# Gated delta rule layer: another partition order for the triangular solver, and the static product's first chunk one place later on TensorE

## The reference, cut to what matters

```python
# x: (8, 2048, 256); 16 heads of 16; W: (256, 256); FFN hidden 768, int weights / 127
x_act = tanh(x)
static_out = einsum('bld,ed->ble', x_act, W)
q = k = to_heads(x_act); v = to_heads(static_out)
# per head: S = lam*S; u = beta*(v_t - S^T k_t); S += k_t u^T; o_t = S^T q_t
y = static_out + o
x = layernorm(x + layernorm(y) * ln_gamma + ln_beta)
x = layernorm(x + ffn(x))          # ffn: (silu(x Wg) * (x Wu)) Wd
```

## Time and profile before

| | before |
|---|---|
| runs | 1788.28, 1783.09, 1778.01 us; median 1783.09 us |
| profiled execution | 1788.68 us, of which the span from first to last instruction is 1786.9 us |
| VectorE busy | 1401.8 us, 78% of the span |
| TensorE busy | 1389.4 us, 78% |
| ScalarE busy | 1104.0 us, 62% |
| GpSimd busy | 793.8 us, 44% |
| mean granted TensorE clock | 0.845 |
| DMA | 190.98 MB in 701069 packets |

### The profile page before, as it was taken

One profiled execution on the slowest core, in us unless ns is written; L12 is line 12 of the kernel. 1 busy time (PEld: TensorE's weight loads), 2 busy tenths in 40 slices (PEclk: granted clock), 3 DMA queues, 4 the chain that ended last, 5 costly groups with the idle time before them and its releaser, 6 DMA issues.

```text
span 1786.9 us, 53677 instructions
## 1 busy us (share of the span) xinstructions
PE 1389.4 (78%) x21032; PEld 1077.5 (60%) x21032; DVE 1401.8 (78%) x3461; ACT 1104.0 (62%) x2357; POOL 793.8 (44%) x1106
## 2 busy tenths in 40 slices
PE   4357878888878888888888888788888887788764
PEld 3245666666666666666666666666666666666542
DVE  5478878878878888888878888888888887888741
ACT  3236667666667666666666666667666666666544
POOL 6023454444444454444444444444453444445442
PEclk9657888878888898888888988889888888989877
DMA  5555545545555555555445556654555554455200
GB/s 122 104 107 112 110 114 118 109 99 114 121 105 116 112 112 110 115 125 125 102 115 115 108 103 121 121 108 114 114 106 107 122 121 105 113 117 106 58 24 24
DMA packets 701069, 190.98 MB, mean 107 GB/s; under 512 B 620688, under 2 KB 688272, under 8 KB 700816
## 3 DMA queue, kind: packets, MB, share of 16 engines
q1 hardware_dynamic: 700816, 187.56, 49.9%
HBM read 103.55 MB, written 67.11 MB: 96 GB/s over the span
## 4 chain that ended last, share of the span: by engine, by line
PE 31%; SPq 20%; DMA 16%; DVE 15%; ACT 9%; issue 6%; POOL 1%; ACTq 0%; POOLq 0%; DVEq 0%
PE pc L181 10%; PE pd L278 5%; SPq L948 5%; SPq L957 4%; SPq L991 4%; DMA scr_t<-t 4%; PE pu L252 4%; PE pf L215 4%; PE pg L252 3%; SPq L1004 3%; DMA scr_x<-xt 3%; ACT v L684 3%; PE pf L226 2%; DMA y_out<-v 2%; DMA scr_g<-gs 2%
## 5 line engine op out<-in xcount | busy, mean ns | idle before, releaser
L885 POOL TENSOR_TENSOR hlo<-gate,hhi 128x512 f16<-128x512 f32 x192 | 228.6, 1193 | 326.8 <-ACT hhi L716 326.4
L181 PE MATMUL pc<-R,tb 128*128 128x32 f16 x4096 | 158.1, 189 | 153.8 <-DVE R L368 135.0
L181 PEld LDWEIGHTS pc<-R,tb 128*128 128x128 f16 x4096 | 147.5, 118 | 172.1 <-DVE R L368 149.6
L181 PE MATMUL pc<-S,e 128*128 128x32 f16 x4096 | 157.3, 187 | 66.4 <-DVE S L389 66.2
L181 PEld LDWEIGHTS pc<-S,e 128*128 128x128 f16 x4096 | 151.9, 118 | 83.2 <-DVE S L389 75.4
L278 PE MATMUL pd<-wd_t,hhi 128*128 128x256 f16 x768 | 176.9, 277 | 13.6 <-DVE xr L487 8.1
L181 PEld LDWEIGHTS pc<-U,kb 128*128 128x128 f16 x4096 | 154.1, 118 | 51.5 <-DVE U L376 49.1
L215 PEld LDWEIGHTS pf<-xb,e 128*128 128x128 f16 x4096 | 152.3, 117 | 46.8 <-DMA e<-scr_x 28.7
L181 PE MATMUL pc<-U,kb 128*128 128x32 f16 x4096 | 159.6, 190 | 25.5 <-DVE U L376 25.5
L278 PE MATMUL pd<-wd_t,hlo 128*128 128x256 f16 x768 | 176.7, 276 | 0.0
L215 PE MATMUL pf<-xb,e 128*128 128x32 f16 x4096 | 156.3, 192 | 23.3 <-DMA e<-scr_x 21.6
(11 more groups left out here) (124 smaller groups left out, 3281.9 us busy)
## 6 DMA issues: line engine op xcount, KB each, us to landing
xa<-L_attn_x SPq DMA_DIRECT2D x128, 128.0 KB
scr_x<-xt SPq DMA_DIRECT2D x64, 256.0 KB, 2.1
xb<-scr_x SPq DMA_DIRECT2D x256, 64.0 KB, 2.9
e<-scr_x SPq DMA_DIRECT2D x256, 64.0 KB, 3.6
scr_g<-gs SPq DMA_DIRECT2D x32, 512.0 KB
gh<-scr_g SPq DMA_DIRECT2D x32, 512.0 KB, 3.9
kb<-k SPq DMA_DIRECT2D x512, 32.0 KB, 2.2
scr_t<-t SPq DMA_DIRECT2D x64, 256.0 KB, 4.4
```

Of the source, the lines that this page charges most:

```text
L181: last = pe.matmul(pc2[:, :, cols], stationary(h, a), moving[:, :, cols], start=a == 0, stop=a == 1)
L885: pool.tensor_tensor(hlo[:, t, :], gate[:, t % 2, :], hhi[:, t, :], ALU.subtract).then_inc(SEM["hl"], 1)
```

## The change

Three edits, one for each of these:

- `scr_g` is laid out (h, b, i, t) in place of (i, b padded to 9, h, t). The store of the gram then writes 16 runs of 256 bytes from each of 128 partitions where it wrote one run of 4096 bytes; the load reads one run of 4096 bytes for each of 128 partitions where it read 16 runs of 256 bytes. The solver's partitions now hold (h, b) in place of (b, h).
- `scr_t` follows this order: (h, b, j, t) in place of (b, h, j, t). Its store stays contiguous. Its loads still read 256 runs of 128 bytes each, the heads now 16 KB apart and not 2 KB.
- On TensorE `pe_static_out` of chunk 0 moves behind `pe_keys_by_state` of chunk 1.

```diff
-        scr_g = nc.dram_tensor("scr_g", [C, B + 1, H, T], F32).ap()[:, 0:B]
-        scr_t = nc.dram_tensor("scr_t", [2, B, H, C, T], F16).ap()
+        scr_g = nc.dram_tensor("scr_g", [H, B, C, T], F32).ap()
+        scr_t = nc.dram_tensor("scr_t", [2, H, B, C, T], F16).ap()
...
+            if live(s):
+                pe_keys_by_state(pe, s, p, 1)
             if live(s + 1):
                 pe_static_out(pe, s + 1, 1 - p, 0)
-            if live(s):
-                pe_keys_by_state(pe, s, p, 1)
-            if live(s + 1):
                 pe_static_out(pe, s + 1, 1 - p, 1)
...
-            sp.dma_start(scr_g.rearrange("i b h t -> b i (h t)"),
-                         gs[:, :, :, :].rearrange("p h j n -> p (h j n)")).then_inc(SEM["gd"], 16)
+            sp.dma_start(scr_g.rearrange("h b i t -> (b i) h t"),
+                         gs[:, :, :, :].rearrange("p h j n -> p h (j n)")).then_inc(SEM["gd"], 16)
...
-            sp.dma_start(gh[:, :, :, :].rearrange("p i j n -> p i (j n)"),
-                         scr_g.rearrange("i b h t -> (b h) i t")).then_inc(SEM["gh"], 16)
+            sp.dma_start(gh[:, :, :, :].rearrange("p i j n -> p (i j n)"),
+                         scr_g.rearrange("h b i t -> (h b) (i t)")).then_inc(SEM["gh"], 16)
...
-            sp.dma_start(scr_t[g].rearrange("b h j t -> (b h) (j t)"),
+            sp.dma_start(scr_t[g].rearrange("h b j t -> (h b) (j t)"),
...
-                             scr_t[g, b].rearrange("h j t -> j h t")).then_inc(SEM[f"tb{g}"], 16)
+                             scr_t[g, :, b].rearrange("h j t -> j h t")).then_inc(SEM[f"tb{g}"], 16)
```

More of the change, by code:

```diff
@@ L324, in pe_step @@
                 pe_down(pe, s - 2, p, 1, range(3, 6))
-            if live(s + 1):
-                pe_static_out(pe, s + 1, 1 - p, 0)
             if live(s):
@@ L329, in pe_step @@
             if live(s + 1):
+                pe_static_out(pe, s + 1, 1 - p, 0)
                 pe_static_out(pe, s + 1, 1 - p, 1)
```

## The result

| | before | changed |
|---|---|---|
| median of the runs of this comparison | 1784.69 us (1778.01 to 1788.28) | 1756.62 us (1754.71 to 1760.27) |
| profiled execution | 1788.68 us | 1760.27 us |
| span | 1786.9 us | 1758.5 us |

The ratio is 0.9843, with a 95% interval of 0.9803 to 0.9882: 28 us or 1.6% faster. The forecast was 1766 us, 17 us faster, with a range of 1752 to 1788. The direction and the place were right; the gain was two thirds larger than forecast, near the fast end of the range.

What follows compares the result with a forecast made beforehand. It took a loop of dependences through four engines, SyncE's queue and DMAs, none full, as the bound. TensorE's 9 plus the store's 8 us, 17 off the profiled 1788.7 (0.95%), put the 1783.1 median at 1766 us, range 1752 to 1788.

Steps and rivals of the forecast that it cites:

- TensorE's edit: Chunk 1's keys by state starts earlier, saving VectorE 0.69 us in 17 rounds; 12.5 us at most, 9 us taken.
- The gram's store: On SyncE, store lands after 4.5 us, not 6.07, and the gram's load issues 2.0 us earlier; 8 us gained.
- The sum: Whole kernel: 9 us from TensorE and 8 us from the gram's store, 17 us together, giving 1766 us.
- both edits at work: Whole kernel: the order on TensorE and the store both gain; 1766 us, own range 1753 to 1774, chance 0.56.
- The load and the inverse's transfers: DMAs: gram's load at worst 4.0 us of data against 2.4 but issued 2.0 us earlier; inverse's transfers cost nothing.
- (b): SyncE's loop over loads of the inverse and `kb` takes back TensorE's gain, only the start is faster: 1778, chance 0.16.
- (c): Gram's store: 256-byte writes cost twice the reads, 38 ns; it lands at 7.0 us, leaving TensorE's 9 us: 1774, chance 0.14.
- (d): Gram's store: small writes at 32 KB pitch cost 57 ns or more, landing after 9.4 us, SyncE waits: 1822, chance 0.08.
- (e): Static product or gram's load in the way of something unseen: within 0.5% of before, 1783, chance 0.06.
- "Under 10 us" for VectorE's wait: Sign of being right: VectorE's wait for TensorE at R falls from 21.0 us to under 10 over the program.
- x and gram would nearly cease to be waited for: Sign of being right: ScalarE's 8.8 us wait for x and VectorE's 8.6 us for the gram all but vanish.
- the growth of the waits for `kb` and scaled keys: Sign of being wrong: these waits grow by what TensorE has won.

Runs made afterwards that it cites:

- the residual moved: SyncE's four loads of the residual put behind the two stores of the inverse: 1739.47 us on the changed kernel, 1767.67 us on the kernel before.
- the new stores: The changed kernel's store and that of the changed kernel with scr_g laid out (b, i, h, t), 4 KB rows, outer count 128; the latter took 1755.48 us.
- the padded pitch: The changed kernel with the heads of scr_g 36 KB apart in place of 32 KB: 1756.06 us, ratio 0.9841.

## Why the prediction was right in direction and two thirds too small

**TensorE's edit.** The mechanism is as forecast: the idle 0.69 us of VectorE in front of chunk 1's R are gone in every round, and in the round shown the static product fits into the wait for R and inverse by rest is not held. The term was taken as three quarters of 12.5 us, 9, whatever SyncE did. It is not a number of its own: 4.5 us on the old layouts, 15 on the new, more than the "12.5 us at most", and with the residual moved 7.7 on the old layouts and again 15 on the new. The reason that the prediction gave for the discount, transfers that do not hang on this loop and come late, is what the runs show on the old layouts. It failed in applying the discount to a kernel whose other edit takes just this away.

**The gram's store.** Only part of SyncE's stretched issue went. The prediction took its figures from one round, which was slower than most (7.29 us from store to gram's load, median 6.93), and said 2.0 us; by the medians the gram's load comes 0.9 us earlier, and the 8 loads take 5.25 us where under 5 were said. The cost of a small write was right at its lower end. The fixed part was too high: the store lands in 3.28 us where 4.5 were said. The old store's stretch was split as 4.0 us of data and 2.1 fixed from an average packet on 8 engines. By its packets, the data lasted 4.4 us, because the early packets were long, and the time before the first packet and behind the last was 1.6; the new stores have 1.3 and 1.2 us there, and 2.0 and 1.4 us of data. The gain was taken as 8 us, nothing of it for the gram and the output in the steady rounds; the layouts alone gave 12.8, with 20.3 us less waiting for the three. The lead that did this was 0.9 us in the median round, not 2.0.

**The sum.** The parts alone, 17.3 us, are the 17 that were forecast, but that is luck: one term was 9 where 4.5 was measured, the other 8 where 12.8 was. The step that failed is the adding of two terms, each priced with the other side left as it was: some 10.7 us come only from both. The prediction had that interaction only as a loss. That 1756.62 us still lies in its own range for both edits at work (1753 to 1774) is so because the fast end of the range took the waits for gram and output in.

**The load and the inverse's transfers.** No loss shows, as forecast: VectorE waits for the gram once, at the start, and the loads of the inverse land after a median of 2.0 us where it was 2.1. The new layout of the inverse was not run alone, so that it costs or gains nothing is argued from this landing time.

**The rivals.** (b), that the other loop takes TensorE's gain back, is true of the order alone, but for the transfers behind the gram's store and not those of inverse and `kb`. (c) and (d) fall by the 17.9 ns of a write, (d) also by the padded pitch, and (e) by the 28 us. The prediction took two rules from the Trainium skill, page "DMA: Bandwidth & Descriptors". With that on the number of engines (section "Why a DMA increments its semaphore by 16 and not by 1") the trace agrees: 8 packets in flight for the old store, 16 or more for the new ones. That on transfers below 512 bytes (section "Specifications"), which the engine is said to read, modify and write, does not show as one read more for each write, since a write of 256 bytes costs no more than a read of it. That such rows are slower for their bytes does show: 256 bytes in 17.9 ns are 14 bytes a ns, 4 KB in 159 ns are 26.

**The signs.** "Under 10 us" for VectorE's wait was nearly met, 10.8, and all of what is left but a few tenths stands in the other chunks. That x and gram would nearly cease to be waited for was right. Of the signs of being wrong, the growth of the waits for `kb` and scaled keys came in part: 4.8 us together, where TensorE's order won some 15.

## What to carry to other kernels

Where several engines and a queue of transfers run in loops of nearly the same length, the price of an edit is not a property of the edit: an order on TensorE was worth 4.5 us or some 15 depending on a transfer elsewhere. So price a change of several parts twice, each part with the others undone and with them done, and look in the waits for what grows when one falls. Read a gain per round from the median of the rounds and not from one pair: the pair shown here had twice the usual lead. In a queue that waits for its own stores to land, put transfers that nobody needs soon into that wait, not in front of the store: here it was worth 17 us for moving four lines.

## What the runs showed of the hardware

Of two transfers of the same bytes and the same row length, one landed in 6.07 us and the other in 2.58. The slow one had an outer count of 8 and 8 packets in flight, the other an outer count of 128 and 16; the slow one's first 44 packets also took 0.37 us each on the average, where its last 57 took 0.16 and so did the other's. Behind the slow store the 8 loads took a median of 5.97 us to issue, behind the two fast ones 4.81 and 5.25. Rows of 256 bytes were written to DRAM at 17.9 ns each, 2048 of them in 3.28 us from issue to landing. Why the early packets were long, whether by the stepping of the DRAM side or otherwise, and by what the store held SyncE up, stays open.
